# An eight-dimension attention stream on one Trainium2 core: keys laid in place by twelve DMAs per pair, both heads' maximum read as one, GpSimd steps held until Vector's small steps are past

## The reference

```
x = x + _L0_attn_ref(_layernorm(x), ...)    # RMS norm, rotary q and k, causal mask, then a SwiGLU
x = x + _L0_xattn_ref(_layernorm(x), ctx, ctx, ...)
x = x + _L1_xattn_ref(_layernorm(x), ctx, mask, ...)   # k masked where j > cumsum(mask)[i]
x = x + _L3_xattn_ref(_layernorm(x), ctx, ctx, ...)
# each:
score = jnp.einsum('bhqd,bhkd->bhqk', q, k) / jnp.sqrt(8)
attn = jax.nn.softmax(score, axis=-1)
out = jnp.einsum('bhqk,bhkd->bhqd', attn, v)
```

## Time and profile before

| what | us |
|---|---|
| median of 3 runs | 3032.33 |
| the profiled execution, its own time | 3037.95 |
| its span, first to last instruction | 3036.1 |
| PE busy in the span | 2081.0 |
| DVE busy | 1662.4 |
| ACT busy | 1013.1 |
| POOL busy | 222.3 |

### The profile page before, as it was taken

The page is one execution under the profiler, slowest core; times in us unless marked ns, Lnnn a source line. Parts: engine busy times, 40 slices in busy tenths (PEclk is TensorE's granted clock), DMA queues, the critical chain, the costliest instruction groups (busy, mean ns, idle before and its releaser), DMA issues. The chain is left out here.

```text
span 3036.1 us, 39171 instructions
## 1 busy us (share of the span) xinstructions
PE 2081.0 (69%) x12768; PEld 1151.9 (38%) x12854; DVE 1662.4 (55%) x5877; ACT 1013.1 (33%) x1920; POOL 222.3 (7%) x251
## 2 busy tenths in 40 slices
PE   4998679728874469982332677777698887569932
PEld 1554323315543325541122444444454444323310
DVE  3765357644444446557667656665633333437754
ACT  1454246521111135532200344443332222126621
POOL 3320032000000041100000000000000000021100
PEclk9998889959986679995555898998898988569965
DMA  1000010000000000000000100000000000000000
GB/s 64 2 2 2 0 42 2 8 0 0 0 6 0 0 25 2 1 11 0 36 0 0 78 3 3 3 3 3 8 1 0 0 0 5 0 7 1 2 1 14
DMA packets 8183, 25.51 MB, mean 8 GB/s; under 512 B 640, under 2 KB 3712, under 8 KB 7040
## 3 DMA queue, kind: packets, MB, share of 16 engines
q1 hardware_dynamic: 8064, 23.93, 2.3%
HBM read 22.88 MB, written 1.05 MB: 8 GB/s over the span
## 5 line engine op out<-in xcount | busy, mean ns | idle before, releaser
L412 DVE TENSOR_REDUCE L_xattn_nmax<-ps 128x2 f32<-128x512 f32 x384 | 259.5, 688 | 197.2 <-PE ps L605 194.2
L524 ACT ACTIVATE L_xattn_probs<-ps 128x1024 f32<-128x1024 f32 x192 | 196.5, 1024 | 129.3 <-PE ps L642 128.9
L678 PE MATMUL ps<-L_xattn_parts,lay 128*128 128x512 bf16 x517 | 167.2, 416 | 23.2 <-POOL L_xattn_parts L295 8.6
L2072 ACT ACTIVATE wide_pr<-wide_sc,wide_nm 128x256 f32<-128x256 f32 x256 | 127.9, 500 | 132.7 <-DVE wide_nm L2024 111.6
L1129 DVE SCALAR_TENSOR_TENSOR moe_z_sb<-ps,weights,moe_a_sb 128x512 f32<-128x512 f32 x64 | 47.7, 750 | 173.8 <-ACT moe_a_sb L1147 173.7
L605 PE MATMUL ps<-L_xattn_ks,L_xattn_qs 64*128 64x256 bf16 x768 | 132.7, 274 | 6.7 <-issue 5.1
L2020 DVE CUSTOM_DVE_ANT_0 wide_sc<-ps,wide_mask 128x256 f32<-128x256 f32 x256 | 97.1, 416 | 67.2 <-PE ps L2112 67.2
L1181 PE MATMUL ps<-moe_z_sb,weights 128*128 128x512 f32 x256 | 123.6, 628 | 8.9 <-DVE moe_z_sb L1129 8.9
L657 PE MATMUL ps<-L_xattn_probs,L_xattn_v 128*32 128x256 f32 x1536 | 122.7, 391 | 2.7 <-ACT L_xattn_pv L535 2.7
L2123 PE MATMUL ps<-const,wide_pr 128*128 128x128 f32 x512 | 90.0, 302 | 36.9 <-DVE wide_pr L2030 36.9
L2112 PE MATMUL ps<-wide_k,wide_q 64*128 64x256 f32 x512 | 71.9, 405 | 45.3 <-DVE wide_nm L2024 37.8
(11 more groups left out here) (491 smaller groups left out, 4618.9 us busy)
## 6 DMA issues: line engine op xcount, KB each, us to landing
weights<-in_packed_L_ffn SPq DMA_DIRECT2D x2, 2608.0 KB, 12.3
weights<-in_packed_L_xattn SPq DMA_DIRECT2D x2, 1316.0 KB, 7.4
wide_mask<-in_mask SPq DMA_DIRECT2D x8, 256.0 KB, 2.7
weights<-in_packed_L_ffn SPq DMA_DIRECT2D x1, 1540.5 KB, 10.1
weights<-in_packed_L_ffn SPq DMA_DIRECT2D x1, 1540.0 KB, 6.7
const<-in_packed_const SPq DMA_DIRECT2D x1, 1165.5 KB, 8.3
weights<-in_packed_L_xattn SPq DMA_DIRECT2D x6, 192.5 KB, 2.5
weights<-in_packed_L_attn SPq DMA_DIRECT2D x2, 576.5 KB, 8.3
```

The lines of the kernel that those rows point to most:

```text
L412: v.tensor_reduce(nm, ps[:, BANK_M + j, :].rearrange("p (t n) -> p t n", t=2), AX.X, ALU.max, negate=True).then_inc(S("m_used"), 1)
L524: a.activation(probs[:, s % RING, :, :, :].rearrange("p j t n -> p j (t n)"), ps[:, BANK_P:BANK_P + 2, :], ACT.Exp, scale=HD ** -0.5)\
L678: mm = pe.matmul(ps[:, SIDE[bank], :], C.lay[:, n, part, gp * P:(gp + 1) * P], parts[:, n, part, :], start=part == 0, stop=part == 2)
L2072: ins = a.activation(pr[:, h % 2, qt, :], sc[:, h % 2, qt, :], ACT.Exp, bias=nm[:, h % 2, qt:qt + 1], accum_out=sums[:, h % 2, qt:qt + 1])
```

## The change

All of it is in `attend8` and in what it is fed.

1. Keys. PE no longer lays k, and ACT no longer copies it. When k's three parts are ready, SyncE issues twelve DMAs per pair, each from 64 partitions of `parts` to 8 rows of `ks`. So that the parts of eight heads lie where a DMA can take them, the columns of the key weights and bias are permuted on the host (`by_rows`), and S0's tables of cosines for k likewise. The ones in the key rows are filled once per stage by two DVE memsets of 32 partitions x 8192 elements, and PE and ACT wait for them at the start of a stage (`CLEARED` is 5 or 6 in place of 3 or 4). `max_scores` waits once per pair for all twelve DMAs. The q lays are one per place, in places 8 to 15 (9 to 16 in S0), all through one PSUM bank.
2. Maximum. `max_scores` does both heads, their matmuls alternating; `maximum` is one reduction over both banks (in S0 two), and `m_used` and `m_ready` count slots. On PE `prob_scores(s - 2)` now follows `max_scores(s + 1)`; the values' steps are one slot later. On DVE `add_max` comes ahead of the high part.
3. GpSimd. Its steps are one per place, and each waits for the low part of the slot before (`beside_maximum`). The normalisation of x moves to ACT (four activations of 128x128 with a scale and a bias, in S0 eight), for which DVE makes one more 128x4 value. In S2 the ranks and the mask come later than the normalisation.
4. In S0 the four rotary products are single 512-column steps through one bank, in four places.

The diff, cut to its core:

```diff
-        LAY = {4: [(1, 0, 0)], 5: [(1, 1, 0)], 7: [(1, 2, 0)], 8: [(0, 0, 0)], 9: [(0, 1, 0)],
-               10: [(0, 2, 0), (1, 3, 1)], 11: [(0, 3, 0), (1, 4, 1)], 12: [(0, 4, 0), (1, 5, 1)],
...
+    Q_LAY = 9 if rope else 8
...
+                sp.wait_ge(S("cleared"), CLEARED)
+                for m in range(PAIRS):
+                    sp.wait_ge(S("k_parts"), m + 1)
+                    if m >= 2:
+                        sp.wait_ge(S("p_ready"), WINDOW * (m - 1))
+                    for part_slot, part in enumerate(K_PARTS):
+                        for j in range(2):
+                            r0 = 64 * j + HD * part_slot
+                            sp.dma_start(kk[r0:r0 + HD, m % 2, :, :], parts[half[j], 1, part, :])\
+                              .then_inc(S("k_laid"), 16)
...
+                def beside_maximum(p):
+
+                    if 0 < p.tau <= SLOTS:
+                        g.wait_ge(S("maxs_ready"), p.tau)
...
+                    stages = [(remainder, 2, 1, 1), (second, 3, 1, 1), (third, 4, 1, 1),
+                              (remainder, 5, 1, 0), (second, 6, 1, 0), (third, 7, 1, 0)]
...
+                    for stage, t, ahead, n in stages:
+                        m = p.job(t, ahead)
+                        if m is not None:
+                            beside_maximum(p)
+                            stage(m, n)
...
+                    yield v.scalar_tensor_tensor(shift, one[:, :, 0], -1.0, first, ALU.mult, ALU.mult)\
+                        .then_inc(S("rstd_ready"), 1)
...
+                def maximum(s):
+                    v.wait_ge(S("m_ready"), s + 1)
+                    nm = nmax[:, s % 2, :, :]
...
+                        v.tensor_reduce(nm, ps[:, BANK_M:BANK_M + 2, :].rearrange("p j (t n) -> p j t n", t=2), AX.X,
+                                        ALU.max, negate=True).then_inc(S("m_used"), 1)
...
+                    v.memset(kk[64 * j + 32:64 * j + 64, :, :, :], 1.0).then_inc(S("cleared"), 1)
...
+                    if 0 <= s - 1 < SLOTS:
+                        add_max(s - 1)
+                    next(side, None)
+                    g, odd = divmod(s - 8, 2)
+                    if odd or not 0 <= g < SLOTS // 2:
+                        g = None
+                    if g is not None:
+                        inverted = invert(g)
+                    if 0 <= s < SLOTS:
+                        v.wait_ge(S("m_used"), s + 1)
+                        high = L.tick(v.tensor_copy(rows_of(s)[:, :, :, AUG], nmax[:, s % 2, :, :]))
+                    next(side, None)
+                    if g is not None:
+                        normalise(g, inverted)
+                    next(side, None)
+                    if 0 <= s < SLOTS:
+                        L.upto(high)
+                        v.tensor_tensor(rows_of(s)[:, :, :, AUG + 1], nmax[:, s % 2, :, :], rows_of(s)[:, :, :, AUG],
+                                        ALU.subtract).then_inc(S("maxs_ready"), 1)
...
-                    if n:
-                        a.activation(kk[:, m % 2, gp, :], ps[:, SIDE[bank], :], ACT.Identity, bias=C.c("aug"))\
-                         .then_inc(S("k_ready"), 1)
-                    else:
-                        a.activation(qs[:, m % 2, gp, :], ps[:, SIDE[bank], :], ACT.Copy).then_inc(S("q_ready"), 1)
...
+                        ins = a.activation(xn[:, (m * PT if rope else 0) + t, :],
+                                           C.x[:, m * PAIR + t * D:m * PAIR + (t + 1) * D], ACT.Identity,
+                                           bias=rstd[:, m % 2, 2, t:t + 1], scale=rstd[:, m % 2, 0, t:t + 1])
...
+                    if s % WINDOW < GP:
                         pe.wait_ge(S("q_ready"), GP * m + gp + 1)
-                        pe.wait_ge(S("k_ready"), GP * m + gp + 1)
+                    if s % WINDOW == 0:
+                        pe.wait_ge(S("k_laid"), 192 * (m + 1))
...
-                        pe.wait_ge(S("m_used"), 2 * (s - 1) + j + 1)
...
+                        pe.wait_ge(S("m_used"), s)
...
-                            mm = pe.matmul(ps[:, bank, c + c0:c + c1], qs[half[j], m % 2, gp, q0:q0 + P],
-                                           kk[half[j], m % 2, gp, b * SEQ + c0:b * SEQ + c1], start=not masked,
-                                           stop=True, skip_group_check=masked)
+                            for j in range(2):
+                                mm = pe.matmul(ps[:, BANK_M + j, c + c0:c + c1], qs[half[j], m % 2, gp, q0:q0 + P],
+                                               kk[half[j], m % 2, gp, b * SEQ + c0:b * SEQ + c1], start=not masked,
+                                               stop=True, skip_group_check=masked)
...
+                            for part in range(3):
+                                mm = pe.matmul(ps[:, BANK_A, :], C.lay[:, 0, part, gp * P:(gp + 1) * P],
+                                               parts[:, 0, part, :], start=part == 0, stop=part == 2)
+                                if part < 2:
+                                    yield
+                            yield mm.then_inc(S("q_laid"), 1)
...
                     if 0 <= s - 1 < SLOTS:
                         turn_max(s - 1)
-                    if 0 <= s - 2 < SLOTS:
-                        prob_scores(s - 2)
-                    g, kt = divmod(s - 4, 2)
+                    g, kt = divmod(s - 5, 2)
                     if 0 <= g < SLOTS // 2:
                         weigh_values(g, kt)
                     next(side, None)
                     if 0 <= s + 1 < SLOTS:
-                        max_scores(s + 1, 0)
-                    next(side, None)
-                    next(side, None)
-                    if 0 <= s + 1 < SLOTS:
-                        max_scores(s + 1, 1)
+                        max_scores(s + 1)
+                    if 0 <= s - 2 < SLOTS:
+                        prob_scores(s - 2)
                     for _ in side:
...
+def by_rows(wt):
+
+    return np.ascontiguousarray(wt.reshape(wt.shape[0], HEADS // 2, 2, HD).transpose(0, 2, 3, 1)).reshape(wt.shape)
```

More of the change, by code:

```diff
@@ L267, in attend8 @@
         slot = lambda s: (s // WINDOW, s % WINDOW // GP, s % GP)
-        places = [Place(tau, WINDOW, PAIRS) for tau in range(-2 * WINDOW, SLOTS + 11)]
+        places = [Place(tau, WINDOW, PAIRS) for tau in range(-2 * WINDOW, SLOTS + 12)]
         with C.turn() as block:
@@ new lines, in _ @@
+                if rope:
+                    stages = [(rotate, 15, 2, 1), (first, 0, 1, 1), (remainder, 1, 1, 1), (second, 2, 1, 1),
+                              (third, 3, 1, 1), (rotate, 4, 1, 0), (first, 5, 1, 0), (remainder, 6, 1, 0),
+                              (second, 7, 1, 0), (third, 8, 1, 0)]
+                else:
+                    stages = [(remainder, 2, 1, 1), (second, 3, 1, 1), (third, 4, 1, 1),
+                              (remainder, 5, 1, 0), (second, 6, 1, 0), (third, 7, 1, 0)]
@@ L351, in _, with newton @@
                 L = Link(v, S("vector_step"))
-                def newton(out, var, n, last):
+                def newton(out, var, n, done=None):
                     a, vv = C.nwt[0][:, 0:n], C.nwt[1][:, 0:n]
@@ L393, in prepare @@
                     L.settle()
-                    first, second = rstd[:, m % 2, 0, :], rstd[:, m % 2, 1, :]
-                    yield from newton(first, one[:, :, 1], PT, not rope)
+                    first, second, shift = (rstd[:, m % 2, n, :] for n in range(3))
+                    yield from newton(first, one[:, :, 1], PT)
+                    yield v.scalar_tensor_tensor(shift, one[:, :, 0], -1.0, first, ALU.mult, ALU.mult)\
+                        .then_inc(S("rstd_ready"), 1)
                     if rope:
@@ L428, in _ @@
                     s = p.tau
-                    m = p.job(2 if rope else 10, 2)
+                    if boundary is not None:
+                        m = p.job(4, 1)
+                        if m is not None:
+                            side = ranks(m)
+                    m = p.job(0 if rope else 4, 2)
                     if m is not None:
-                        side = prepare(m)
+                        side = itertools.chain(side, prepare(m))
                     if 0 <= s < SLOTS:
-                        maximum(s, 0)
+                        maximum(s)
@@ L541, in _ @@
[L541 to L546 removed]
+                            a.wait_ge(S("q_laid"), GP * m + gp + 1)
+                            a.activation(qs[:, m % 2, gp, :], ps[:, BANK_A, :], ACT.Copy).then_inc(S("q_ready"), 1)
@@ L673, in turn_values, with project @@
                     mm.then_inc(S("pv_turned"), 1)
-                def lay(m, n, gp, bank):
-                    pe.wait_ge(S(("q_parts", "k_parts")[n]), m + 1)
-                    for part in range(3):
-                        mm = pe.matmul(ps[:, SIDE[bank], :], C.lay[:, n, part, gp * P:(gp + 1) * P],
-                                       parts[:, n, part, :], start=part == 0, stop=part == 2)
```

(5 more changed lines are left out.)

411 lines of the change are left out of this document (200 added, 211 removed).

## The result

The changed kernel took 3067.5 us (median of 4 runs), the kernel before 3035.5 in the same rounds: a ratio of 1.011, 95% interval 1.008 to 1.014. It is slower by 1.1%, and I had forecast 2974. The profiled execution has a span of 3067.0 us and its own time is 3068.9, so 30.9 us of span are to be explained. Medians in this document are those of undisturbed executions; one of experiment 4's six took 6282 us and is left out.

What follows compares the result with a forecast made beforehand. PE was taken to bound slots with lays, DVE those without. Slots -73 and starts +15.5 us gave -58, so 3032.3 became 2974; the forecast's own range was 2950 to 3000, the whole range 2915 to 3025.

Steps and rivals of the forecast that it cites:

- Lays and pairing: S1's full window: six lay slots 17.3 us in place of 19.3, the other ten -2.6, a window -4.6.
- the new loop: Places 10 to 15: scores, exponentials, ScalarE's copies, then TensorE's lay and maximum scores; 2.97 or 2.67 us, mean 2.82.
- DVE is the bound: Slots without lays: maximum, high, add and low run end to end on DVE, 2.10 us per slot.
- The last pairs: Each stage's last pair gets shorter: S1 -1 us, S2 -6, S0 -5.5.
- Rival 1: Slots: PE alone is the bound and the loop over ACT hides; stages lose 110 us, time 2938; 22%.
- The fills: Stage starts: two DVE memsets of 8192 elements ahead of the statistics, 0.85 ns per element, 14.0 us for both.
- rival 2: Stage starts: fills go two elements at a time, 7 us less per stage, 2946 us; 13%.
- Starts: Time to each stage's first maximum: S1 and S3 +6.5 us each, S0 +7, S2 -4.5, together +15.5.
- Ends: Stretch from each stage's last low part to the next stage's first statistics: 0 us change in all four stages.
- keys by DMA: Twelve key DMAs per pair, issued by SP some 0.4 us each, covered in slots and at starts; priced at nothing.
- GpSimd's waits: GpSimd's steps waiting for low parts cost nothing; the gain from shorter small DVE steps was counted inside the slots.
- Rival 3: Slots: both heads' maximum as one gate leaves DVE idle; at 0.3 us per slot +77, 3051 us; 12%.

Runs made afterwards that it cites:

- experiment 4: The kernel before, with only its probability scores moved from the head to the end of TensorE's slot: 3218.7 us, ratio 1.059.
- experiment 1: The changed kernel with the probability scores first in TensorE's slot again: 2976.8 us, ratio 0.980 to the kernel before.
- experiment 3: The changed kernel, TensorE's order kept, with ScalarE copying the weighed values one slot sooner: 3000.6 us, ratio 0.989 to the kernel before.
- experiment 2: The changed kernel with TensorE's order maximum scores, weighing, probability scores: 3056.6 us, ratio 1.006 to the kernel before.
- experiment 7: The changed kernel with the fills of ones written as half as many four-byte elements: 3033.9 us, ratio 0.998 to the kernel before.
- experiment 8: The changed kernel with the probability scores first and the fills written as four-byte elements: 2935.2 us, ratio 0.967 to the kernel before.
- experiment 5: The changed kernel with probability scores first and each head's maximum taken by itself, with its own gate and reduction: 3003.4 us, ratio 0.990 to the kernel before.

## Why the prediction was wrong

- **Lays and pairing: S1's window right, by two errors that cancel.** S1's full windows shrank by 4.6 as said: the six lay slots take 16.6 us for 17.3 predicted, the other ten gave 1.8 for 2.6; six of S2 take 23.0 for 23.0. But the path that I gave the lay slots was not the one they waited on: q's copy held PE for 0.55 us in the six, the values' copy for 2.51, and they alternate between 3.16 and 2.37 to 2.57, not 3.0 and 2.7. That the size agrees is in part luck. S0's three windows and last pair went +0.8, -3.1, -9.7 and +1.9, for -3.5, -7.5, -7.5 and -5.5.
- **The step that failed: where the new loop holds.** I named it (scores last, exponentials, ScalarE's copy, TensorE) but followed it only through q's copy, and so gave it places 10 to 15. In the same ScalarE queue the values' copy stands behind the same exponentials, and the weighing waits for it in every second slot of every pair. "DVE is the bound" in slots without lays was then wrong: in S1's last pair it is busy for 77% (90% before), and in S2's, where PE was full, PE has 81%. The last pairs went +3.0 and +4.4 (S1, S2) for -1 and -6 predicted; in S2's window the other ten slots gave 1.2 us for 5.3. Experiments 1, 3 and 4 show it from both sides. The path through q's copy exists as well, behind the first: in experiments 2 and 3, with the values' copy mostly out of the way and the scores still late, the lay matmul waits 68.2 and 53.0 us for it. Of what was run, only early scores open both.
- **Without that loop** the slots give -122.5 us. Rival 1 had -110 for this, the better estimate of the two. That experiment 1 lands 3 us from my 2974 is chance: its slots are 50 below my terms, its starts 27 and its ends 7 above, and the rest of the program 12 longer.
- **The fills: mis-sized.** I took the duration of a row (2.62 us for 3072 elements) as its cost. Its row also says that 0.6 us of "issue" stood ahead: 3.2 us in all, 1.05 ns per element, 17.1 for both fills. Measured: 17.3, where I had 14.0. The Trainium skill (page "VectorE: DVE Perf Modes", section "Zero memsets can be issued as uint32 (trn2)") has one cycle per element whatever the type; with that page's clock of 0.96 GHz this makes an estimate of 17.1 for both. The distances of this trace agree with the Trainium skill, and the duration in my row does not. Two-byte elements do not go two at a time (rival 2 falls), and experiment 7 shows the count of elements to be what costs, also for ones.
- **Starts.** S1 and S3 came 4.5 and 4.8 above the forecast: 3.7 are the later statistics, 1 the chain behind them, which gave back 2.8 where I had 3.9. S2 came 5.6 above, 3.6 of it the fills. S0 missed by 11; with the fills moved it is still +6. Its timeline shows the second pair's turns, projections and rotations now among the first pair's lays, whose first six copies of q span 14.9 us, where S1's take 10.8 (2.15 each). No run tried that reading, and what S0's start lost stays open.
- **Ends: left out.** +17.4; +7 in experiment 1, +2.3 in experiment 8. The values' steps stand one slot later and the scores last, but part is the clock: with the same code behind the slots, S0's end took 19.5 us here at a mean granted clock of 0.64 and 17.0 in experiment 7 at 0.84, S3's 23.9 at 0.72 and 27.0 at 0.58. How much each has was not separated.
- **Priced at nothing, rightly:** keys by DMA, though SyncE issues one every 0.66 us and not every 0.4. GpSimd's waits, taken away, cost 19 us in the slots, where I expected a small gain of them. Rival 3's gate costs less than pairing gains (experiment 5), and its reduction is one link of the ring; I put that at 1.22 us with no working (my 0.08 off twice 0.68 would be 1.28), and 1.22 is what it takes.

## What to carry to other kernels

When a block moves to the end of an engine's slot, take every consumer of its result, and on the consumer's engine every instruction queued behind it, and follow each to where it is waited for; one path through q's copy was not all of them. If the busiest engine's share falls while slots get longer, look for a ring and sum one turn of it from the timeline. Price an instruction by the distance to its neighbour, with the "issue" ahead of it, and not by its duration alone.
